# Attention and ternary feed-forward layer on one core: the order of sixteen matmuls inside each half of the probabilities-times-values product

## The chip, the cores and the metric

The kernel runs on one core of one Trainium2 chip. The metric is device time in microseconds (us) of one execution. Besides the plain timed executions there is one execution recorded by the hardware profiler, and every row below is from it. The engines are named as the profile names them: PE is TensorE (matmuls), PEld its loading of stationary operands, DVE is VectorE, ACT is ScalarE, POOL is GpSimd, and SP issues the DMAs.

## What is computed

The input x is 2048 rows of 256. It is normalised by layernorm, and the output is x plus an attention over it plus a feed-forward layer over it:

```
xn = layernorm(x)
qkv = einsum('bsd,ed->bse', xn, Wqkv)            # 16 heads of 128, q, k and v
logits = einsum('bqhd,bkhd->bhqk', q, k) * 128 ** -0.5
w = softmax(logits)
out = einsum('bhqk,bkhd->bqhd', w, v)
attn = einsum('bse,de->bsd', out, Wout)
hidden = sigmoid(xn @ quant(w1).T) * (xn @ quant(w2).T)   # 704 wide, weights -1, 0, 1
result = x + attn + hidden @ quant(w3).T
```

To keep float32 accuracy the operands of the matmuls are split in a high part, rounded to the matmul's type, and a low part, the rest. A product of two split operands is then three matmuls: high by high, high by low, low by high.

## The kernel before, in words

The feed-forward layer comes first and ends about 100 us into the span. Then come the 16 heads, each taking some 112 us. All of the program's order is written out by hand: each engine has its own list of instructions and waits for semaphores of the others.

Inside a head the 2048 queries are 16 tiles of 128 (`t`), and two tiles are a pair (`p`). For one tile PE computes the logits against all 2048 keys in two halves (`logits`, lines 349 to 351, twelve matmuls of 512 columns over the tile). DVE takes the row maximum (line 826), ACT the exponentials (line 629), DVE turns blocks of 32 by 32 (line 836), and DMAs move these blocks so that the keys lie on the partitions. ACT then rounds the high part (line 623) and POOL subtracts for the low part (line 967), both into `parts`. `parts` holds, for each of 16 blocks of 128 keys (`kb`), 256 columns of low parts (index 0) and 256 of high parts (index 1), for the 256 queries of a pair.

The function that the change touches is `products(half)`: it multiplies the values by the probabilities for half of the keys, that is 8 of the blocks. For each block it issues one matmul of 512 columns, `v_hi` by low and high parts together (line 357, into `ps_pv`, one whole bank of PSUM), and one of 256 columns, `v_lo` by the high parts alone (line 359, into `ps_pv_hi`, the second half of the same bank). Every one has its own stationary operand, so each matmul is preceded by a weight load. The last of the sixteen raises the semaphore `s_pv`, for which ACT waits before it reads the product (line 615) and before it writes the next pair into the same half of `parts` (line 623).

PE's list, which is what sets the order around the change, repeats every two tiles:

- at an odd tile: logits (12 matmuls), the output projection of an earlier pair (lines 367 to 369, six matmuls of 256 columns), and the first half's products of the next pair;
- at an even tile: logits (12), at one of them also a values projection ahead of the products (line 339, six matmuls), then the second half's products, and at most of them a projection of queries or values behind it (lines 329 and 339, six matmuls of 512 columns).

So `products` is called 256 times: 16 heads, 8 pairs, 2 halves. Half of the calls follow matmuls of 512 columns and half follow the six of 256 columns. Each head but the last ends with the next head's keys (line 320, 24 matmuls of 512 columns).

Of the kernel before, what the change touches and what calls it, by code (L numbers as in the profile page):

```python
# [43 lines left out]
KH = HALF // P  # L44
# [24 lines left out]
def build(nc, x_d, wqkv_d, wo_d, w1_d, w2_d, w3_d, out_d):  # L69
    ctx = ExitStack()  # L70
    with ctx:
# [242 lines left out]
        def _(pe):  # L314
# [40 lines left out]
            def products(half):  # L355
                for kb in range(half * KH, half * KH + KH):
                    nc.tensor.matmul(ps_pv, v_hi[:, kb, :], parts[:, kb].rearrange("p s a q -> p (s a q)"),  # L357
                                     start=(kb == 0), stop=False, skip_group_check=True)
                    last = nc.tensor.matmul(ps_pv_hi, v_lo[:, kb, :], parts[:, kb, 1].rearrange("p a q -> p (a q)"),  # L359
                                            start=False, stop=(kb == T - 1), skip_group_check=True)  # L360
                last.then_inc(s_pv, 1)
# [83 lines left out]
            def product_step(h, p, half, first=False):  # L445
                pe.wait_ge(s_pl, count(16, h, 2 * p + half + 1))
                if half == 0 and (p >= 1 or not first):
                    pe.wait_ge(s_olo, count(8, h, p))
                if p == 0:
                    pe.wait_ge(s_vlo, count(2, h, half + 1))  # L450
                products(half)
# [584 lines left out]
```

## Time and profile before

| | |
|---|---|
| median of 3 executions | 1926.77 us (1925.68 to 1930.1) |
| the profiled execution, its own time | 1927.86 us |
| span in the profile, first to last instruction | 1926.0 us |
| PE busy | 1874.0 us, 97% |
| DVE busy | 1648.2 us, 86% |
| POOL busy | 1359.7 us, 71% |
| ACT busy | 1253.0 us, 65% |
| DMA, mean busy share | 66.6% of 16 engines |

The span is 1.86 us shorter than that execution's time. A matmul's own duration in the profile (0.40 us for 512 columns, 0.28 us for 256) overlaps the next one's, since matmuls are pipelined. What a matmul costs in a stream is the distance from its start to the start of the next one, its pitch. The timeline shows starts to 0.01 us, so pitches are best read over several matmuls.

### The profile page before, as it was taken

The page shows a single profiled execution, that of the slowest core. Times are in us where ns is not written, and L with a number is a line of the kernel's source. Part 1 is how long each engine was busy: PE and PEld are TensorE (multiplying, and loading weights), DVE is VectorE, ACT ScalarE, POOL GpSimd, SP SyncE. Part 2 cuts the span into 40 slices and gives each one's busy share as a digit, 9 for nine tenths or more (in the row PEclk, how much of TensorE's full clock was granted, in tenths as well). Part 3 has the DMA queues.
Part 4 walks back from the last instruction along what each step waited for, and adds up shares of the span by engine and source line. Part 5 has one row for each costly group of instructions (what it writes and reads, how often), then busy time and mean ns, then how long its engine had stood idle before and what let it go on. Part 6 is the DMA issues. An engine that isn't in the chain of part 4 may idle for free.

```text
span 1926.0 us, 29406 instructions
## 1 busy us (share of the span) xinstructions
PE 1874.0 (97%) x9508; PEld 1582.4 (82%) x9508; DVE 1648.2 (86%) x2216; ACT 1253.0 (65%) x1698; POOL 1359.7 (71%) x514
## 2 busy tenths in 40 slices
PE   5979999999999999999999999999999999999997
PEld 4858888888888888888888888888888888888885
DVE  6368898898989899898989989898998989899894
ACT  3446676666767676666767666676766667666663
POOL 2418687776868777686878768686876768687676
PEclk9999999999999999999999999999999999999998
DMA  3036677676767767676776767677676767767675
GB/s 105 1 90 159 157 167 177 152 170 159 171 157 173 172 151 172 159 168 159 166 179 151 171 159 169 159 163 182 148 173 157 170 161 163 175 148 177 148 165 141
DMA packets 197108, 300.70 MB, mean 156 GB/s; under 512 B 38144, under 2 KB 57280, under 8 KB 197056
## 3 DMA queue, kind: packets, MB, share of 16 engines
q1 hardware_dynamic: 197056, 300.11, 66.6%
q8 instruction: 20, 0.33, 0.1%
q14 instruction: 32, 0.26, 0.0%
HBM read 12.65 MB, written 2.10 MB: 8 GB/s over the span
## 4 chain that ended last, share of the span: by engine, by line
PE 88%; SPq 3%; DVE 3%; POOL 2%; ACT 1%; DMA 1%; issue 1%; DVEq 0%; POOLq 0%; ACTq 0%
PE ps_o L357 23%; PE ps_o L359 12%; PE ps_s L349 11%; PE ps_s L351 11%; PE ps_s L350 11%; PE ps_t L339 4%; PE ps_s L320 4%; PE ps_t L329 4%; SPq L266 3%; PE ps_s L392 2%; PE ps_o L367 1%; PE ps_o L369 1%; PE ps_o L368 1%; POOL parts L967 1%; DVE prob L836 1%
## 5 line engine op out<-in xcount | busy, mean ns | idle before, releaser
L967 POOL TENSOR_TENSOR parts<-raw,parts 128x2048 fp32r<-128x2048 f32 x256 | 1185.3, 4631 | 454.6 <-ACT parts L623 453.8
L629 ACT ACTIVATE prob<-ps_s,neg_max 128x1024 f32<-128x1024 f32 x512 | 567.0, 1114 | 471.2 <-DVE neg_max L830 471.2
L357 PE MATMUL ps_o<-parts,v_hi 128*128 128x512 f32 x2048 | 739.7, 399 | 8.7 <-POOL parts L967 5.1
L826 DVE TENSOR_REDUCE row_max<-ps_s 128x1 f32<-128x1024 f32 x512 | 612.3, 1212 | 71.0 <-PE ps_s L351 51.6
L836 DVE STREAM_TRANSPOSE prob<-prob 128x1024 f32<-128x1024 f32 x512 | 604.3, 1218 | 58.5 <-ACT prob L629 58.0
L359 PE MATMUL ps_o<-parts,v_lo 128*128 128x256 f32 x2048 | 578.0, 282 | 0.0
L623 ACT CAST parts<-raw 128x2048 fp32r<-128x2048 f32 x256 | 490.5, 1916 | 99.7 <-DMA raw<-prob 96.4
L357 PEld LDWEIGHTS ps_o<-parts,v_hi 128*128 128x128 f32 x2048 | 387.8, 189 | 99.9 <-POOL parts L967 6.1
L349 PE MATMUL ps_s<-k_hi,q_hi 128*128 128x512 f32 x1024 | 404.0, 395 | 12.6 <-ACT prob L629 11.8
L351 PE MATMUL ps_s<-k_hi,q_lo 128*128 128x512 f32 x1024 | 400.3, 391 | 0.0
L350 PE MATMUL ps_s<-k_lo,q_hi 128*128 128x512 f32 x1024 | 399.8, 390 | 0.0
L359 PEld LDWEIGHTS ps_o<-parts,v_lo 128*128 128x128 f32 x2048 | 387.5, 189 | 4.3
L349 PEld LDWEIGHTS ps_s<-k_hi,q_hi 128*128 128x128 f32 x1024 | 192.5, 188 | 63.4 <-ACT prob L629 11.5
L351 PEld LDWEIGHTS ps_s<-k_hi,q_lo 128*128 128x128 f32 x1024 | 192.6, 188 | 42.7
L350 PEld LDWEIGHTS ps_s<-k_lo,q_hi 128*128 128x128 f32 x1024 | 192.8, 188 | 36.2
L853 DVE SCALAR_TENSOR_TENSOR y<-ps_o,inv_denom,y 128x256 f32<-128x256 f32 x256 | 111.0, 475 | 3.4 <-PE ps_o L369 3.4
L629 ACT ACTIVATION_READ_ACCUMULATOR prob<-ps_s,neg_max 128x1 f32 x512 | 99.3, 194 | 0.0
L329 PE MATMUL ps_t<-xt_hi,w_sp 128*128 128x512 f32 x256 | 90.5, 394 | 0.0
L339 PE MATMUL ps_t<-xt_hi,w_sp 128*128 128x512 f32 x256 | 90.1, 393 | 0.0
L840 DVE TENSOR_TENSOR o_lo<-ps_o,o_hi 128x256 fp32r<-128x256 f32 x128 | 54.3, 424 | 40.9 <-ACT o_hi L615 28.6
L320 PE MATMUL ps_s<-xt_hi,w_sp 128*128 128x512 f32 x256 | 81.8, 390 | 0.0
L367 PE MATMUL ps_o<-wo_hi,o_hi 128*128 128x256 f32 x256 | 72.3, 283 | 5.0 <-DVE o_lo L842 5.0
(94 smaller groups left out, 1599.1 us busy)
## 6 DMA issues: line engine op xcount, KB each, us to landing
raw<-prob SPq DMA_DIRECT2D x2048, 128.0 KB, 2.4
v_raw<-v_turned SPq DMA_DIRECT2D x244, 64.0 KB, 2.0
w_raw<-wqkv_dram SPq DMA_DIRECT2D x32, 128.0 KB, 2.5
y<-x_dram SPq DMA_DIRECT2D x4, 512.0 KB, 5.8
wo_raw<-wqkv_dram SPq DMA_DIRECT2D x16, 128.0 KB, 2.5
wo_raw<-wo_dram SPq DMA_DIRECT2D x16, 128.0 KB, 2.3
out_dram<-y SPq DMA_DIRECT2D x8, 256.0 KB, 2.9
w_raw<-w_dram SPq DMA_DIRECT2D x2, 704.0 KB, 10.1
```

Of the source, the lines that this page charges most:

```text
L329: last = nc.tensor.matmul(dst, w_sp[:, 0, c, w, :], x[:, c, col], start=(n == 0), stop=(n == 3 * C - 1))
L339: last = nc.tensor.matmul(dst, w_sp[:, 2, c, w, :], x[:, c, j * 512:(j + 1) * 512], start=(n == 0), stop=(n == 3 * C - 1))
L349: nc.tensor.matmul(ps_s[:, bank, :], q_hi[:, qb, tile], k_hi[:, col], start=True, stop=False)
L350: nc.tensor.matmul(ps_s[:, bank, :], q_hi[:, qb, tile], k_lo[:, col], start=False, stop=False)
L351: last = nc.tensor.matmul(ps_s[:, bank, :], q_lo[:, qb, tile], k_hi[:, col], start=False, stop=True)
L357: nc.tensor.matmul(ps_pv, v_hi[:, kb, :], parts[:, kb].rearrange("p s a q -> p (s a q)"), start=(kb == 0), stop=False, skip_group_check=True)
L359: last = nc.tensor.matmul(ps_pv_hi, v_lo[:, kb, :], parts[:, kb, 1].rearrange("p a q -> p (a q)"), start=False, stop=(kb == T - 1), skip_g ...
L623: nc.scalar.copy(half_of(1, half), moved(p, half)).then_inc(s_ph, 1)
L629: nc.scalar.activation(prob[:, t % E_RING, half * HALF:(half + 1) * HALF], ps_s[:, 2 * half:2 * half + 2, :].rearrange("p b n -> p (b n)") ...
L826: nc.vector.reduce_max(row_max[:, t, half:half + 1], ps_s[:, 2 * half:2 * half + 2, :].rearrange("p b n -> p (b n)"), AX_X).then_inc(s_mx, 1)
L836: nc.vector.transpose(tile, tile).then_inc(s_xp, 1)
L967: nc.gpsimd.tensor_tensor(half_of(0, half), moved(p, half), half_of(1, half), ALU.subtract).then_inc(s_pl, 1)
```

## The change

Inside one call of `products` the same sixteen matmuls are issued in another order: the loop over the eight blocks is now two loops. All eight of line 357 come first, then all eight of the former line 359, now line 360. The semaphore is still raised by the last one, the waits stand ahead of the first one as before, and nothing else in the program is changed; the lines behind it move down by one.

```diff
                 for kb in range(half * KH, half * KH + KH):
                     nc.tensor.matmul(ps_pv, v_hi[:, kb, :], parts[:, kb].rearrange("p s a q -> p (s a q)"),
                                      start=(kb == 0), stop=False, skip_group_check=True)
+                for kb in range(half * KH, half * KH + KH):
                     last = nc.tensor.matmul(ps_pv_hi, v_lo[:, kb, :], parts[:, kb, 1].rearrange("p a q -> p (a q)"),
                                             start=False, stop=(kb == T - 1), skip_group_check=True)
                 last.then_inc(s_pv, 1)
```

On PE, in the first head, the end of an output projection, then the start of a call of `products` before the change:

```order
L367 MATMUL ps_o<-wo_hi,o_hi 128x256
L368 MATMUL ps_o<-wo_lo,o_hi 128x256
L369 MATMUL ps_o<-wo_hi,o_lo 128x256
L357 MATMUL ps_o<-parts,v_hi 128x512 [waits output_low_ready,pt_low_ready]
L359 MATMUL ps_o<-parts,v_lo 128x256
L357 MATMUL ps_o<-parts,v_hi 128x512
L359 MATMUL ps_o<-parts,v_lo 128x256
```

The same place with the change, where x7 and x8 are equal instructions in a row and all lines from 359 on are one higher:

```order
L368 MATMUL ps_o<-wo_hi,o_hi 128x256
L369 MATMUL ps_o<-wo_lo,o_hi 128x256
L370 MATMUL ps_o<-wo_hi,o_lo 128x256
L357 MATMUL ps_o<-parts,v_hi 128x512 [waits output_low_ready,pt_low_ready]
L357 MATMUL ps_o<-parts,v_hi 128x512 x7
L360 MATMUL ps_o<-parts,v_lo 128x256 x8
L349 MATMUL ps_s<-k_hi,q_hi 128x512 [waits exponentials_ready,queries_low_ready]
```

The sixteen stand between the same neighbours and behind the same wait; only their inner order has moved. On DVE, ACT, POOL and SP no instruction has moved.

## Rows read from the trace of the kernel before

**Rows 1.** The page's first part: busy time, share, count of each engine.
```profile
PE 1874.0 (97%) x9508; PEld 1582.4 (82%) x9508; DVE 1648.2 (86%) x2216; ACT 1253.0 (65%) x1698; POOL 1359.7 (71%) x514
```

**Rows 2.** Windows; busy us (count) of PE, PEld, DVE, ACT, POOL; clock, DMA.
```profile
165.00:820.00 655.00, 654.54 (x3333) 553.85 (x3332) 585.07 (x775) 444.55 (x599) 482.42 (x176) 1.00 0.71 164
820.00:1800.00 980.00, 979.12 (x4987) 828.21 (x4986) 875.18 (x1159) 663.34 (x894) 726.85 (x263) 1.00 0.71 165
```

**Rows 3.** Waits of PE: total us, times, longest us.
```profile
PE ps_s L349 <- ACT prob L629: 11.8, 7, 3.0
PE ps_o L357 <- POOL parts L967: 5.1, 3, 2.5
PE ps_o L367 <- DVE o_lo L842: 5.0, 3, 2.3
```

**Rows 4.** Groups by line, 165 to 1820 us: busy us, mean ns; idle before.
```profile
L357 PE MATMUL ps_o<-parts,v_hi 128*128 128x512 f32 x1899 | 680.7, 397 | 0.5 <-POOL v_lo L960 0.5
L826 DVE TENSOR_REDUCE row_max<-ps_s 128x1 f32<-128x1024 f32 x474 | 566.8, 1212 | 63.1 <-PE ps_s L351 45.0
```

**Rows 5.** Timeline of PE, a call behind 512 columns: start us, duration us, what.
```profile
864.72 0.39 PE L357 MATMUL ps_o<-parts,v_hi 128*128 128x512 f32 x1
864.95 0.28 PE L359 MATMUL ps_o<-parts,v_lo 128*128 128x256 f32 x1
865.07 0.39 PE L357 MATMUL ps_o<-parts,v_hi 128*128 128x512 f32 x1
865.30 0.28 PE L359 MATMUL ps_o<-parts,v_lo 128*128 128x256 f32 x1
...
867.54 0.39 PE L329 MATMUL ps_t<-xt_hi,w_sp 128*128 128x512 f32 x1
```

**Rows 6.** Timeline of PE, a call behind the output projection.
```profile
872.36 0.40 PE L357 MATMUL ps_o<-parts,v_hi 128*128 128x512 f32 x1
872.60 0.28 PE L359 MATMUL ps_o<-parts,v_lo 128*128 128x256 f32 x1
...
873.07 0.39 PE L357 MATMUL ps_o<-parts,v_hi 128*128 128x512 f32 x1
873.30 0.28 PE L359 MATMUL ps_o<-parts,v_lo 128*128 128x256 f32 x1
...
875.18 0.39 PE L349 MATMUL ps_s<-k_hi,q_hi 128*128 128x512 f32 x1
```

**Rows 7.** Timeline of PE between them: ninth 512-column matmul, first of 256 columns.
```profile
869.38 0.39 PE L351 MATMUL ps_s<-k_hi,q_lo 128*128 128x512 f32 x1
...
871.65 0.28 PE L367 MATMUL ps_o<-wo_hi,o_hi 128*128 128x256 f32 x1
```

**Rows 8.** Timeline of PE, feed-forward: 48 of 256 columns, then 48 of 512.
```profile
60.56 0.28 PE L403 MATMUL ps_t<-w_q,hid_hi 128*128 128x256 f32 x1
...
66.25 0.39 PE L392 MATMUL ps_s<-xt_hi,w_q 128*128 x1
...
77.30 0.28 PE L403 MATMUL ps_t<-w_q,hid_hi 128*128 128x256 f32 x1
```

**Rows 9.** Timeline of the weight loads, output projection.
```profile
872.00 0.19 PEld L368 LDWEIGHTS ps_o<-wo_lo,o_hi 128*128 128x128 f32 x1
872.12 0.19 PEld L369 LDWEIGHTS ps_o<-wo_hi,o_lo 128*128 128x128 f32 x1
```

**Rows 10.** Timeline of ACT: the exponential ahead of the logits at 875.18.
```profile
873.36 1.12 ACT L629 ACTIVATE prob<-ps_s,neg_max 128x1024 f32<-128x1024 f32 x1 [1.50 <-DVE neg_max L830]
```

**Rows 11.** Timeline of PE, keys (24 of line 320) from first to the next line.
```profile
99.73 0.40 PE L320 MATMUL ps_s<-xt_hi,w_sp 128*128 128x512 f32 x1
...
105.19 0.39 PE L329 MATMUL ps_t<-xt_hi,w_sp 128*128 128x512 f32 x1
...
888.40 0.39 PE L320 MATMUL ps_s<-xt_hi,w_sp 128*128 128x512 f32 x1
...
893.88 0.39 PE L349 MATMUL ps_s<-k_hi,q_hi 128*128 128x512 f32 x1
```

## The prediction

> **What bounds the kernel now.** I read the busy shares first, then a table of long windows, then who waits for whom, and last the timeline of PE, matmul by matmul.
>
> PE is busy 97% of the span, DVE 86% [rows 1]. From 165 to 1800 us the reader is to see that PE is busy 1633.66 of 1635 us, with its clock granted in full, while DVE is busy 585.07 of 655 and 875.18 of 980 us, 89% in both [rows 2]. PE's waits for other engines are few: 7, 3 and 3 of them, 21.9 us together [rows 3], and of all that only 0.5 us stands before line 357 between 165 and 1820 us [rows 4]. So over 85% of the span there is one bound: the sum of PE's pitches. A busy share of 97% alone would not prove that, since matmul records overlap; what proves it is that the starts follow each other without a hole. The question is therefore whether the order of sixteen matmuls changes their pitches, and it has to be read from starts, not from durations.
>
> **The change part by part.** It removes no matmul, adds none, moves no wait, no semaphore and no DMA. The one term is the time of a call of `products`, and there are two kinds of call.
>
> Before, a call behind 512-column matmuls runs from 864.72 to 867.54, 2.82 us [rows 5], and one behind the output projection from 872.36 to 875.18, again 2.82 us [rows 6]. Both are eight pairs of 512 and 256 columns, 0.353 us a pair.
>
> What do the two widths cost in streams of their own? Between the two calls stand eighteen matmuls of 512 columns. From the ninth, at 869.38, to the first of 256 columns at 871.65 there are ten pitches in 2.27 us, 0.227 us each [rows 7]. The eight ahead of those, directly behind the alternating group, take 869.38 - 867.54 = 1.84 us, 0.230 us each [rows 5, 7]. So behind 256-column work the long ones need some time to settle at 0.227. The six of 256 columns take 872.36 - 871.65 = 0.71 us, 0.118 us each [rows 6, 7]; the 48 of the feed-forward layer take 66.25 - 60.56 = 5.69 us, 0.1185 us each [rows 8]. A pair in streams costs 0.227 + 0.118 = 0.345 us and in alternation 0.353 us: alternating costs about 8 ns a pair. It is the 512-column matmul that pays it: in the rows it stands at 0.23 to 0.24 us and the short one at 0.12.
>
> The new call behind 512-column matmuls: the stream before it is already settled, so 8 x 0.227 = 1.816, and 8 x 0.1185 = 0.948, together 2.764 us. Saved: 2.82 - 2.764 = 0.056 us.
>
> The new call behind the output projection: the eight long ones come right behind 256-column work, so I take the unsettled 0.230, 1.84 us, and 0.948 again, 2.788 us. Saved: 0.032 us.
>
> The two together are 0.088 us every two tiles, 0.044 us a call on average. Not every call counts. Between 165 and 1820 us there are 1899 matmuls of line 357, 237 calls [rows 4], where PE has no cover. The other 19 lie in the first and last head, where PE waits for others [rows 3] and what it saves may only lengthen a wait. I count them as nothing; in full they would be 0.8 us. The sum is 237 x 0.044 = 10.4 us.
>
> Bounds of that term. The trace shows no stream of line 357, so its pitch there is bounded by rows of others. The high end: the 48 matmuls of 512 columns in the feed-forward layer stay at 0.230 us (77.30 - 66.25 = 11.05 us) and never settle lower [rows 8]. With 0.230 in both kinds of call each saves 0.032, together 7.6 us. The low end: 0.227 in both kinds saves 0.056 a call, 13.3 us. To that may come something behind the call: 24 key matmuls behind a stream of 256 columns take 105.19 - 99.73 = 5.46 us, and behind an alternating group 893.88 - 888.40 = 5.48 us [rows 11]. So the work behind a call may settle 0.02 us sooner, for 237 calls 4.7 us; with it the low end is 18 us. I take nothing for it, because 0.02 us is the difference of two single readings to 0.01 us.
>
> Do eight short matmuls in a row expose their weight loads? A load is recorded at 0.19 us, longer than the pitch of 0.12 us, and the next load starts 0.12 us after it [rows 9]. So a load's record is a latency that overlaps, and streams of short matmuls with a new load each already run at 0.118 [rows 6 to 8]. I charge nothing. All eight short ones add into the same 256 columns; the output projection does so three in a row, within that same 0.118.
>
> Is there cover that goes away? The nearest deadline is the exponential that the next tile's logits wait for. It ended at 873.36 + 1.12 = 874.48, and the logits started at 875.18 [rows 10, 6]: 0.70 us to spare, against some 0.06 us that PE comes earlier. DVE is late next, but it still waits for PE's logits, 45.0 us in 165 to 1820 us [rows 4], which over 118 pairs of tiles is 0.38 us each, more than 0.088. The waits of PE itself, 21.9 us, stay.
>
> The sum stands against the profiled execution: 1927.86 - 10.4 = 1917.5 us. That execution lies 1.09 us above the median of the runs shown, 1926.77, so what I predict for a median is 1916.4 us.
>
> **The rivals.**
>
> The pitch belongs to line 357, not to the order. Its matmuls read `parts` and load `v_hi`, which no other line does, and in the alternating group most stand at 0.235 us. If they do so in a row, a call is 8 x 0.235 + 0.948 = 2.828 us, and 256 calls are 2 us longer: 1928.8, no measurable change. For it: that I have no stream of this line. Against it: two of the matmuls in the rows, at 865.07 and 873.07, have a pitch of 0.23 and not 0.24 [rows 5, 6], so the operands don't forbid it. A rule bears on this. The Trainium skill (TensorE: Matmul & The Clock Gate, "Back-to-back issue gap") gives the distance between isolated matmuls at full clock as columns over 2.4 GHz plus 2.5 ns, whatever stands beside them. By that rule a pair would cost 325 ns in any order and the change nothing, 1926.8 us. The rows disagree with its size, 353 ns in alternation, and with its independence, since the streams add up to 345.
>
> DVE takes over. It is busy 89% of the time, and its list is a chain of its own. If its 0.38 us of slack in a pair of tiles is bridged by some other wait, PE's saving turns into a new wait of line 349 for the exponentials, and the time stays at 1926.8. For it: the high share. Against it: DVE's wait for PE comes back at every odd tile, so the two stay in step.
>
> Slower: eight long reads of `parts` in a row. The long matmul directly behind the output projection has the longest pitch of all in the rows, 872.36 to 872.60, 0.24 us [rows 6]. If that is what line 357 costs when the reader before it is not relieved by a short matmul, for instance because ACT and POOL write the other half of `parts` at the time, a call becomes 8 x 0.24 + 0.948 = 2.868 us, 0.048 more, and 256 calls 12.3 us more: 1939.1 us. It turns slower from a pitch of 0.234 us on. Against it: in alternation a long one reads `parts` two thirds of the time already, without a steady 0.24.
>
> **How the numbers follow.** What can be told from no change here is 0.2%, 3.9 us. I give the forecast 0.82, the pitch of the line itself 0.07, DVE taking over 0.05, and the slower case 0.06. The forecast's own range is its bounds, 7.6 to 18 us off the median, 1909 to 1919. The range that should hold the time 8 times in 10 goes a little further on both sides, from 1908.5 to 1922, where part of a gain is swallowed by waits at the heads' ends. The two cases without an effect and the slower one, 0.18 together, are left outside. Faster by over 0.2%: 0.82, within it: 0.12, slower: 0.06.
>
> **What would show each step.** In the timeline of the kernel after, behind 512 columns: eight starts of line 357 at 0.227 us and eight of line 360 at about 0.12, the call 2.76 us long; behind the projection 2.79 us. The window from 165 to 1800 us still has PE busy all the time, with more matmuls in the same 980 us: 4987 now, and 0.5% more is 25. The waits of line 349 stay near 11.8 us. The forecast is wrong if line 357 in a row stands at 0.235 or above, if PE shows new waits for ACT in the middle heads, or if line 360 has a pitch of 0.19, a load laid bare.

## The result: 0.45% faster, by 9.0 us

The changed kernel takes 1917.59 us (median of 6, 1916.14 to 1921.84), the kernel before 1926.59 us (median of 6, 1925.68 to 1930.1). The ratio is 0.9955, with a 95% interval of 0.994 to 0.9969. The prediction was 1916.4 us, from 1908.5 to 1922. The profiled execution of the changed kernel took 1921.41 us, one of the two long ones of the six, and has a span of 1919.6 us. The two profiled executions differ by 6.4 us, not by 9; where the rest lies is shown further down.

The busy times [rows 1] and the longer of the two windows [rows 2] of the kernel after, in the same columns:

```profile
PE 1864.8 (97%) x9508; PEld 1573.8 (82%) x9508; DVE 1648.4 (86%) x2216; ACT 1252.9 (65%) x1698; POOL 1356.6 (71%) x514
```
```profile
820.00:1800.00 980.00, 978.19 (x5007) 826.81 (x5006) 878.50 (x1164) 664.87 (x895) 727.27 (x265) 1.00 0.71 165
```

In the same 980 us PE issues 5007 matmuls instead of 4987, 0.4% more. But its idle time there has doubled, from 0.9 to 1.8 us. That is small, and it is the first sign of something that was not in the forecast. The waits of PE [rows 3] show it as well; line numbers from 359 on are one higher:

```profile
PE ps_s L349 <- ACT prob L630: 12.5, 7, 3.0
PE ps_o L357 <- POOL v_lo L961: 5.8, 6, 2.0
```

The wait for the exponentials is about what it was. The one for `v_lo` was in the profile before too, and the forecast passed over it:

```profile
PE ps_o L357 <- POOL v_lo L960: 3.6, 3, 2.0
```

It stood at 3.6 us in 3 places and is now 5.8 us in 6.

Next the timeline of PE for the two kinds of call. Behind 512-column matmuls [rows 5]:

```profile
862.08 2.03 PE L357 MATMUL ps_o<-parts,v_hi 128*128 128x512 f32 x8
863.95 1.08 PE L360 MATMUL ps_o<-parts,v_lo 128*128 128x256 f32 x8
864.87 0.39 PE L329 MATMUL ps_t<-xt_hi,w_sp 128*128 128x512 f32 x1
...
877.99 0.39 PE L339 MATMUL ps_t<-xt_hi,w_sp 128*128 128x512 f32 x1
```

The call takes 864.87 - 862.08 = 2.79 us, before 2.82. The eight long ones take 1.87 us, 0.234 each; the eight short ones 0.92 us, 0.115 each. Behind the output projection [rows 6]:

```profile
869.67 0.40 PE L357 MATMUL ps_o<-parts,v_hi 128*128 128x512 f32 x1
...
872.47 0.39 PE L349 MATMUL ps_s<-k_hi,q_hi 128*128 128x512 f32 x1
```

2.80 us, before 2.82. A full period of two tiles, from one projection to the next, is 877.99 - 864.87 = 13.12 us. The same period of the kernel before, from the row at 867.54 [rows 5] to the next projection, is 13.22 us:

```profile
880.76 0.39 PE L339 MATMUL ps_t<-xt_hi,w_sp 128*128 128x512 f32 x1
```

So 0.10 us went. The rows show starts to 0.01 us, too coarse to say from one period where. Averaged over all periods of this form between 200 and 1760 us (68 in the trace before, 69 after), the period is 13.220 and 13.119 us. Of that difference 0.068 us lies inside the two calls: 2.823 to 2.785 us behind 512 columns, 2.823 to 2.793 us behind the output projection. The other 0.033 us lies in the 30 matmuls of 512 columns behind them. Inside the calls the long matmuls kept their average pitch, 0.234 us in both orders. It is the short ones that became cheaper, from 0.1185 to 0.115 us.

### The profile page after: what moved, and what is told of

It reads as the page before. It is cut to its first block, busy times and chain, and to the rows that moved or that the text cites. A ratio compares the mean times of both kernels' runs of the same rounds, so it can differ in the third digit from the quotient of the medians.

```text
span 1919.6 us, 29406 instructions
## 1 busy us (share of the span) xinstructions
PE 1864.8 (97%) x9508; PEld 1573.8 (82%) x9508; DVE 1648.4 (86%) x2216; ACT 1252.9 (65%) x1698; POOL 1356.6 (71%) x514
## 4 chain that ended last, share of the span: by engine, by line
PE 77%; POOL 6%; SPq 5%; issue 4%; DVE 4%; ACT 2%; DMA 2%; POOLq 0%; DVEq 0%; ACTq 0%
PE ps_o L357 20%; PE ps_o L360 10%; PE ps_s L349 10%; PE ps_s L350 10%; PE ps_s L351 10%; SPq L266 5%; POOL parts L968 5%; PE ps_t L339 4%; PE ps_s L320 4%; PE ps_t L329 4%; PE ps_s L393 2%; DVE prob L837 1%; PE ps_o L368 1%; PE ps_o L370 1%; PE ps_o L369 1%
## 5 line engine op out<-in xcount | busy, mean ns | idle before, releaser
L357 PE MATMUL ps_o<-parts,v_hi 128*128 128x512 f32 x2048 | 527.6, 399 | 10.0 <-POOL v_lo L961 5.8
L357 PEld LDWEIGHTS ps_o<-parts,v_hi 128*128 128x128 f32 x2048 | 376.8, 189 | 96.7 <-issue 6.0
L360 PEld LDWEIGHTS ps_o<-parts,v_lo 128*128 128x128 f32 x2048 | 274.2, 188 | 23.9
L360 PE MATMUL ps_o<-parts,v_lo 128*128 128x256 f32 x2048 | 277.4, 278 | 0.0
```

## The experiments

Each kernel is the changed one with one edit, unless the text says it starts from the one before. Times are medians; the kernel before, run beside them on the same chip, took 1925.5 to 1926.1 us.

**1. The wait for v_lo between the long and the short matmuls.** The reason is the new wait above. It is an edit that the new order makes possible, since the long ones don't read `v_lo`. Only the first pair of a head (`p == 0`) has this wait.

```diff
-            def products(half):
+            def products(half, low_ready=None):
                 for kb in range(half * KH, half * KH + KH):
                     nc.tensor.matmul(ps_pv, v_hi[:, kb, :], ...)
+                if low_ready is not None:
+                    pe.wait_ge(s_vlo, low_ready)
                 for kb in range(half * KH, half * KH + KH):
...
                 if p == 0:
-                    pe.wait_ge(s_vlo, count(2, h, half + 1))
+                    pe.wait_ge(s_vhi, count(2, h, half + 1))
-                products(half)
+                products(half, count(2, h, half + 1) if p == 0 else None)
```

> The changed kernel, but in the first pair of a head the wait for v_lo stands between the eight long matmuls and the eight short ones (ahead of the long ones only v_hi is waited for). Theory C (POOL's burst of parts, v_lo, parts, v_lo, parts, wo_lo at tiles 5 to 7 of every head sets three deadlines, and the faster PE now runs into them, 0.27 us a head): the stalls ahead of line 357 at tiles 5 and 6 go, but POOL still finishes wo_lo at the same moment, so the wait ahead of the output projection at tile 7 grows by about what they gave: 0 to 1 us faster than the changed kernel, 1917 us. Rival P (the pitches alone explain the 9 us, those stalls are no real cover that ran out): the same time as the changed kernel with no new wait anywhere, and the stalls at tiles 5 and 6 stay. Rival Q (each stall costs by itself): 2 to 3 us faster, 1915 us.

Measured: 1917.43 us (5 runs), ratio 0.9955 (0.9941 to 0.9969), the changed kernel's own. To see why, first POOL in the changed kernel, tiles 5 to 7 of one head:

```profile
920.96 4.64 POOL L968 TENSOR_TENSOR parts<-raw,parts 128x2048 fp32r<-128x2048 f32 x1 [2.47 <-ACT parts L624]
925.57 2.41 POOL L961 TENSOR_TENSOR v_lo<-v_raw,v_hi 128x1024 fp32r<-128x1024 f32 x1
927.95 4.61 POOL L968 TENSOR_TENSOR parts<-raw,parts 128x2048 fp32r<-128x2048 f32 x1
932.52 2.39 POOL L961 TENSOR_TENSOR v_lo<-v_raw,v_hi 128x1024 fp32r<-128x1024 f32 x1
...
935.03 4.60 POOL L968 TENSOR_TENSOR parts<-raw,parts 128x2048 fp32r<-128x2048 f32 x1
939.60 0.73 POOL L947 TENSOR_TENSOR wo_lo<-wo_raw,wo_hi 128x256 fp32r<-128x256 f32 x1
```

and PE at the three places that need what POOL makes there:

```profile
928.03 2.13 PE L357 MATMUL ps_o<-parts,v_hi 128*128 128x512 f32 x8
...
935.02 0.68 PE L357 MATMUL ps_o<-parts,v_hi 128*128 128x512 f32 x2
...
940.37 0.39 PE L351 MATMUL ps_s<-k_hi,q_lo 128*128 128x512 f32 x1
940.59 0.38 PE L368 MATMUL ps_o<-wo_hi,o_hi 128*128 128x256 f32 x1
```

POOL works without a pause from 920.96 to past 940.33. It ends `v_lo` at 927.98, and line 357 starts at 928.03, 0.05 us later and 0.20 us behind the matmul before it, instead of 0.12; the second half at 934.91, and line 357 starts at 935.02, where the first of the two has a pitch of 0.29 us instead of 0.234; `wo_lo` at 940.33, and the projection starts at 940.59 with its first matmul at a pitch of 0.22 us instead of 0.12. Three times PE has just been waiting for POOL. In experiment 1 the first two waits are gone, and the third stays:

```profile
935.58 0.76 POOL L949 TENSOR_TENSOR wo_lo<-wo_raw,wo_hi 128x256 fp32r<-128x256 f32 x1
```
```profile
936.19 0.39 PE L351 MATMUL ps_s<-k_hi,q_lo 128*128 128x512 f32 x1
936.56 0.38 PE L370 MATMUL ps_o<-wo_hi,o_hi 128*128 128x256 f32 x1
```

`wo_lo` ends at 936.34 and the projection comes 0.37 us behind the last logits instead of 0.22. What the first two gave, the third took.

**2. All three relieved.** The edit of experiment 1, and POOL makes `wo_lo` before the pair's first subtraction:

```diff
+                    if r == 3:
+                        wo_low(h)
                     if r >= 2:
                         low(h, r - 2, 0)
...
-                    if r == 3:
-                        wo_low(h)
```

> As the run with the wait for v_lo between the loops, and POOL computes wo_lo ahead of the pair's first subtraction at tile 6 instead of behind it. Theory C: all three deadlines of a head are off the path, 0.27 us a head come back, 14 middle heads: 3 to 4 us faster than the changed kernel, about 1914 us, a middle head 110.75 us instead of 111.04. Rival P: the same time as the changed kernel, 1917.6 us, middle head 111.04. Rival Q: the same as the run before it, 1915.

Measured: 1911.7 us (5 runs, 1910.89 to 1912.53), ratio 0.9922 (0.9909 to 0.9936). The gain is larger than expected, 5.9 us and not 3 to 4. No wait of PE is left between 165 and 1770 us. This head took 111.08 us in the changed kernel, from its first key matmul to that of the next head (885.59 to 996.67), and is 110.75 us here (880.18 to 990.93).

The other 2 us are two heads, the second and the last but one, in which POOL's burst ended over 1 us later than in a middle head of the changed kernel, and PE waited for it: 112.09 and 112.27 us there, 111.29 and 111.12 us here. This kernel beats both others.

**3 and 4. Less work for POOL, with the new order and with the old.** Both leave out seven eighths of `v_lo` in all heads but the first, so that part keeps the first head's numbers:

```diff
-            def values_low(h, half):
+            def values_low(h, half, full):
...
+                if not full:
+                    kb = slice(half * KH, half * KH + 1)
```

> The changed kernel in which POOL subtracts only one of eight blocks for v_lo in all heads but the first (the rest of v_lo is left as the first head's): POOL's burst is 4 us shorter per head. Theory C: no stall at tiles 5 to 7 any more, 3 to 4 us faster than the changed kernel, about 1914 us. Rival P: the same as the changed kernel, 1917.6 us.

> The kernel before with the same part of v_lo left out. Theory C: only some 0.06 us of stall a head are there to lose, so 0.5 to 1.5 us faster than the kernel before, 1925.5 us, and the run beside it is 11 to 12.5 us faster than this one: 0.10 us for every two tiles, 8 pairs, 15 heads. Rival P: the difference between the two stays the 9 us of the change.

Measured: 1913.62 us (ratio 0.9935, 0.9921 to 0.9948) with the new order, 1924.28 us (0.999, 0.9981 to 0.9999) with the old. The difference is 10.7 us. In these two the middle heads are all alike, 110.73 against 111.53 us: 0.80 us a head, 8 periods of 0.10. So this is what the order is worth when nothing else binds. With POOL's full work the same head of the two kernels differs by 111.56 - 111.08 = 0.48 us. The cover that ran out costs a middle head 0.3 us.

The sum over the second to the fifteenth head, from the first key matmul of the second to that of the sixteenth, leaves the ends of the program out:

| | order before | order after | difference |
|---|---|---|---|
| all of `v_lo` (before, after) | 1563.1 us | 1557.1 us | 6.0 us |
| an eighth of it (experiments 4, 3) | 1562.0 us | 1551.1 us | 10.9 us |

In experiment 2, with all of POOL's work but in another order, the same 14 heads take 1551.3 us. So in these heads the order was worth 10.9 us, and waits for POOL took some 5 us of it back.

**5. Four long, four short, twice.**

```diff
-                for kb in range(half * KH, half * KH + KH):
+                for quarter in (0, 1):
+                  for kb in range(half * KH + 4 * quarter, half * KH + 4 * quarter + 4):
                     nc.tensor.matmul(ps_pv, v_hi[:, kb, :], ...)
-                for kb in range(half * KH, half * KH + KH):
+                  for kb in range(half * KH + 4 * quarter, half * KH + 4 * quarter + 4):
                     last = nc.tensor.matmul(ps_pv_hi, v_lo[:, kb, :], ...)
```

> The changed order in two portions: four long, four short, four long, four short. If the cost lies in the switching between widths, the call is between both: from 2.79 us towards 2.82, with the four short ones after each switch at 0.122, 0.116, 0.114, 0.113 as in the changed kernel, and the long ones at 0.233 throughout: 2 x (4 x 0.233 + 0.465) = 2.79 us, the same as the changed kernel, since the first short ones are the only dear ones and a switch costs 10 ns. If the long row itself is what pays (eight in a row needed), the call stays at 2.82 us. Time 1918 by the first, 1926 by the second.

Measured: 1918.64 us, ratio 0.9964 (0.995 to 0.9978). The timeline of a call:

```profile
858.77 1.09 PE L358 MATMUL ps_o<-parts,v_hi 128*128 128x512 f32 x4
859.70 0.63 PE L361 MATMUL ps_o<-parts,v_lo 128*128 128x256 f32 x4
860.17 1.09 PE L358 MATMUL ps_o<-parts,v_hi 128*128 128x512 f32 x4
861.10 0.62 PE L361 MATMUL ps_o<-parts,v_lo 128*128 128x256 f32 x4
861.55 0.39 PE L329 MATMUL ps_t<-xt_hi,w_sp 128*128 128x512 f32 x1
```

2.78 us, and the long ones again at 0.93 / 4 = 0.233. Groups of four are enough; a change of width every fourth matmul costs nothing that can be read.

**6 and 7. Other operands for the long matmuls.** The moving one, then the stationary one (the outputs are then other numbers):

```diff
-nc.tensor.matmul(ps_pv, v_hi[:, kb, :], parts[:, kb]...,
+nc.tensor.matmul(ps_pv, v_hi[:, kb, :], xt_hi[:, kb % 2, kb // 2 % 4 * 512:kb // 2 % 4 * 512 + 512],
```
```diff
-nc.tensor.matmul(ps_pv, v_hi[:, kb, :], parts[:, kb]...,
+nc.tensor.matmul(ps_pv, xt_hi[:, 1, kb * P:(kb + 1) * P], parts[:, kb]...,
```

> The changed kernel in which the moving operand of line 357 is 512 columns of xt_hi (the operand of the projections) instead of parts, so the products come from other data. Theory A (the pitch of 0.233 us of line 357 in a row comes from reading parts): it falls to 0.227, the call to about 2.74 us. Theory B (it comes from the weight v_hi or from the place it adds into): it stays 0.233.

> The changed kernel in which the stationary operand of line 357 is 128 columns of xt_hi instead of v_hi, so the products come from other data. Theory A (reading parts sets 0.233 us): the pitch stays 0.233. Theory B (the weight load of v_hi): it falls to 0.227.

Measured (one execution each, 1921.02 and 1919.28 us): with `xt_hi` moving the long ones are at 1.82 / 8 = 0.2275, with `xt_hi` stationary at 1.87 / 8 = 0.234. So the pitch of 0.234 goes with reading `parts`. But the short ones behind the `xt_hi` reads went the other way, from 0.115 to 0.1175. Experiment 6:

```profile
860.28 1.98 PE L357 MATMUL ps_o<-xt_hi,v_hi 128*128 128x512 f32 x8
862.10 1.10 PE L360 MATMUL ps_o<-parts,v_lo 128*128 128x256 f32 x8
863.04 0.39 PE L329 MATMUL ps_t<-xt_hi,w_sp 128*128 128x512 f32 x1
...
876.18 0.39 PE L339 MATMUL ps_t<-xt_hi,w_sp 128*128 128x512 f32 x1
```

The call is down to 2.76 us, and yet the period is 13.14 us, not shorter than 13.12: the logits behind it lost what the call won. Theory A is right on the pitch and useless for the time.

**8. The old order on other operands.** The kernel before with experiment 6's edit.

> The kernel before, alternating, with the moving operand of line 357 replaced by 512 columns of xt_hi (its products come from other data). With the stream of long matmuls on xt_hi this completes the table of order by operand. If alternating itself costs (order), a pair stays near 0.353 us and the call at 2.82 against 2.76 us of the stream on the same operand. If the dear pair came from reading parts (operand), the pair falls to 0.345 and the call to 2.76 in either order.

Measured (one execution): 1919.54 us. The call is 862.56 - 859.76 = 2.80 us, the period 875.70 - 862.56 = 13.14 us.

```profile
859.76 0.39 PE L357 MATMUL ps_o<-xt_hi,v_hi 128*128 128x512 f32 x1
...
862.56 0.39 PE L329 MATMUL ps_t<-xt_hi,w_sp 128*128 128x512 f32 x1
...
875.70 0.39 PE L339 MATMUL ps_t<-xt_hi,w_sp 128*128 128x512 f32 x1
```

Neither expectation fits: the call fell, though not to 2.76, and the period fell nearly all the way. Alternating widths is not dear by itself: on `xt_hi` both orders have the same period. It is dear where both matmuls of a pair read `parts`, and there the short one reads again half of the columns that the long one has just read; whether it is the same tensor or the same columns, no run tells apart.

**9 and 10. `parts` at another place.**

```diff
+        pad = sb("pad", [P, 16])
         parts = sb("parts", [P, T, 2, 8, BLK], F32R)
```
and, for the second, the line of `parts` moved ahead of that of `prob`.

> The changed kernel with parts starting 64 bytes further on in every partition. If the long pitch of 0.233 us comes from how the address of parts stands to that of the weights within a short period, it changes, to 0.227 or to more. If it comes from something else of parts, it stays 0.233 and the time 1917 to 1918 us.

> The changed kernel with parts ahead of prob and raw, 64 KB lower in every partition. If the region of SBUF in which parts lies sets its pitch (the operands that stream at 0.227 us, xt_hi and k_hi, lie low), the long pitch falls towards 0.227. Otherwise 0.233 and 1917 to 1918 us.

Measured (one execution each): 1919.41 and 1918.37 us. 64 KB lower nothing changes (0.234 and 0.115). 64 bytes on, the pitches change, to 0.2275 and 0.119, and the period does not, 874.89 - 861.77 = 13.12 us. So it is reading `parts` where it stands, and not reading it at all, that goes with 0.234:

```profile
859.00 1.98 PE L358 MATMUL ps_o<-parts,v_hi 128*128 128x512 f32 x8
860.82 1.12 PE L361 MATMUL ps_o<-parts,v_lo 128*128 128x256 f32 x8
861.77 0.40 PE L330 MATMUL ps_t<-xt_hi,w_sp 128*128 128x512 f32 x1
...
874.89 0.40 PE L340 MATMUL ps_t<-xt_hi,w_sp 128*128 128x512 f32 x1
```

**11. Short ones first.**

```diff
+                blocks = list(range(half * KH, half * KH + KH))
+                if half == 0:
+                    long(blocks.pop(0))
                 for kb in range(half * KH, half * KH + KH):
                     nc.tensor.matmul(ps_pv_hi, v_lo[:, kb, :], ...)
+                for kb in blocks:
+                    last = long(kb)
...
```

(`long(kb)` issues the 512-column matmul of line 357, whose own loop is gone.)

> The changed kernel with the eight short matmuls ahead of the long ones (in the first half behind the first long one, which has to open the bank). The number of changes of width a call is the same. If the cost is one of changing width, the period of two tiles stays 13.12 us. If it is the settling of long matmuls behind short ones, the logits behind the call start settled (2.72 us for twelve instead of 2.735) but the long ones of the call are unsettled in both kinds of call: within 0.03 us of 13.12 us.

Measured (one execution): 1925.18 us. The call is 2.82 us, the period 865.29 - 852.08 = 13.21 us, nearly all of the gain gone. This was expected by neither.

```profile
852.08 0.40 PE L339 MATMUL ps_t<-xt_hi,w_sp 128*128 128x512 f32 x1
...
862.47 1.10 PE L364 MATMUL ps_o<-parts,v_lo 128*128 128x256 f32 x8
863.41 2.03 PE L357 MATMUL ps_o<-parts,v_hi 128*128 128x512 f32 x8
865.29 0.40 PE L329 MATMUL ps_t<-xt_hi,w_sp 128*128 128x512 f32 x1
```

The long ones are at 0.235 as in the changed kernel, the short ones at 0.1175. They are at 0.115 only where they stand behind long ones that read `parts` at its own place.

**12. The kernel before with `parts` 64 bytes on.** The pad of experiment 9 alone.

> The kernel before, alternating, with nothing changed but that parts starts 64 bytes further on in every partition. Theory S (the dear pair is one of the steady patterns into which loads and matmuls fall, and where operands start decides between them; the order is only one way to leave it): the pair falls from 0.353 to about 0.350 us or less, the period of two tiles from 13.22 to about 13.13 us, the time to about 1918 us like the regrouped kernel. Theory O (alternating widths on parts is dear by itself): 13.22 us and 1926 us, as before.

Measured: 1928.54 us (11 runs), ratio 1.0013 (1.0004 to 1.0022); the period is 877.23 - 864.00 = 13.23 us.

```profile
861.19 0.39 PE L358 MATMUL ps_o<-parts,v_hi 128*128 128x512 f32 x1
...
864.00 0.40 PE L330 MATMUL ps_t<-xt_hi,w_sp 128*128 128x512 f32 x1
...
877.23 0.40 PE L340 MATMUL ps_t<-xt_hi,w_sp 128*128 128x512 f32 x1
```

Theory S falls: moving `parts` does not help the old order. The order does, at both places tried.

In one table, the call behind 512 columns, and the period of two tiles, both in us, each read once. The averages over the 68 or 69 periods between 200 and 1760 us of each trace are within 0.01 us of these:

| order, what the long ones read | call | period |
|---|---|---|
| alternating, parts | 2.82 | 13.22 |
| alternating, parts 64 bytes on | 2.81 | 13.23 |
| alternating, xt_hi | 2.80 | 13.14 |
| short first, parts | 2.82 | 13.21 |
| long first, parts | 2.79 | 13.12 |
| long first, parts 64 bytes on | 2.77 | 13.12 |
| long first, xt_hi | 2.76 | 13.14 |

## Why the prediction was right, and where its steps were not

**The bound** was read rightly: PE's pitches set the time of the middle heads, and the order acts through them, by 0.10 us in each period of two tiles.

**The call** was mis-sized, and the saving in it was put on the wrong matmuls. I took 0.227 for a long one and 0.1185 for a short one from streams of other lines. They are 0.234 and 0.115. The sum let the long ones fall from their pitch in alternation to 0.227; they did not fall, on average 0.234 us in both orders. Nearly all of the saving is the eight short ones, 0.030 us a call, and no row of the kernel before foretold it. By my own reckoning a long one at 0.234 leaves no gain, so that the call gained at all is luck as far as this step goes. The rival that the pitch belongs to line 357 had the long one right, 0.235, and the wrong end, since it kept 0.1185 for the short ones. Saved per call are 0.038 and 0.030 us on average, where I had 0.056 and 0.032.

**Behind the call** I took nothing, and named up to 0.02 us a call as a bound. It is 0.033 us in a period of two calls, inside that bound. So the pitches give 0.10 us a period where the sum had 0.088: 0.020 less than in the sum inside the calls, 0.033 more than in the sum behind them. The two errors nearly cancel.

**The cover** is the step that failed. I asked for the nearest deadline, left out the wait for `v_lo` when I listed PE's waits, looked at the logits' wait for the exponentials (0.70 us to spare, and it did hold), and took that for all of PE's waits. A sum over a repeating period says nothing on a place that comes once a head. There POOL makes `v_lo` twice and `wo_lo` once beside its usual work, and PE was close behind it already. In the kernel before POOL ended the first of the two at 928.41 + 2.41 = 930.82 us, and the call that needs it started at 931.02:

```profile
928.41 2.41 POOL L960 TENSOR_TENSOR v_lo<-v_raw,v_hi 128x1024 fp32r<-128x1024 f32 x1
```
```profile
931.02 0.40 PE L357 MATMUL ps_o<-parts,v_hi 128*128 128x512 f32 x1
```

0.20 us to spare; the second half and `wo_lo` had 0.19 and 0.33 us (937.77 to 937.96 and 943.20 to 943.53). The new order brings PE 0.28 us forward by the first of them: without a wait there, in experiment 1, the call starts 42.34 us behind the head's first key matmul, and before 42.62 us. POOL does not come forward with it: `v_lo` ends 42.42 us behind that matmul before and 42.39 us with the change. Experiment 1 shows that the waits are linked, 2 and 3 what they cost: a middle head gained 0.48 us instead of 0.80, and 14 heads 6.0 us instead of 10.9. The rival on another engine taking over named the wrong engine: I looked at DVE, the busiest after PE at 89%, and it was POOL at 74%. A mean share hides a burst.

**The slower case**, 0.24 us for a long one in a row, did not come: it is 0.234, as in alternation.

**The median and the profile.** From the end of the feed-forward layer's work to the last head's keys the two profiled executions differ by 6.5 us. The first head takes 118.84 us before and 118.28 after. In experiment 5, whose periods are those of the changed kernel, it takes 115.51, and the rows of the windows show the clock beside it, first the changed kernel, then experiment 5:

```profile
108.00:132.00 24.00, 17.58 (x73) 13.21 (x72) 17.73 (x20) 8.33 (x15) 0.93 (x2) 1.00 0.38 90
132.00:152.00 20.00, 12.80 (x44) 9.83 (x44) 16.01 (x17) 12.88 (x17) 11.22 (x4) 0.83 0.68 155
```
```profile
108.00:132.00 24.00, 18.61 (x68) 14.10 (x67) 16.24 (x19) 7.75 (x15) 0.94 (x2) 0.86 0.40 95
132.00:152.00 20.00, 14.54 (x66) 11.20 (x64) 17.85 (x19) 14.00 (x18) 13.11 (x5) 1.00 0.65 150
```

In both, PE waits for the first exponentials in this part, and the granted clock then falls to the half level, 1.2 GHz, for 7 to 8 us in all. Where it comes later, part of it meets the first call of `products`, here the changed kernel, then experiment 5:

```profile
148.02 3.49 PE L357 MATMUL ps_o<-parts,v_hi 128*128 128x512 f32 x8 [2.01 <-POOL v_lo L961]
```
```profile
146.16 1.18 PE L358 MATMUL ps_o<-parts,v_hi 128*128 128x512 f32 x4 [0.53 <-POOL v_lo L962]
```

The next logits start at 152.43 and 149.04 us, so the call takes 4.41 against 2.88 us, and the wait ahead of it is 2.01 against 0.53 us. Together these are the 3 us. They are not set by the order: in the trace of experiment 12, with the old order, the first head took 115.68 us. The same 3 us probably separate the two long executions of the changed kernel, 1921.41 and 1921.84, from the other four, 1916.14 to 1918.02; only one of the six has a trace, so this was not shown. How much of the 9.0 us between the medians is the order, and how much an unequal share of such executions, stays open within that: between 6 and 9 us. So the total, 10.4 us forecast and 9.0 measured, agrees better than its steps do. Pitches right by two errors, a cover left out that cost some 5 us, and up to 3 us that may not be the order's stand between them; the close agreement is partly luck.

**A rule weighed.** The Trainium skill (TensorE: Matmul & The Clock Gate, "Back-to-back issue gap") makes the distance of isolated matmuls depend on their columns alone, an estimate of 216 and 109 ns for these by its formula. No matmul here stands alone, each having its own weight load, and no stream reached that: the least were 0.227 and 0.115 us. And sixteen matmuls of these widths took 2.76 to 2.82 us by order and operand, so the estimate is too low for this kernel and has no place for what the order does.

**What stays open** is why reading `parts` by both matmuls is dear in one order and not in the other, why the short ones are the cheaper for it, and why a saving inside the call can come back behind it (experiments 6 and 9). The runs show the table, not the mechanism: a shift by 64 bytes and the number of width changes do not decide, and what stands ahead of a short matmul does. No run took the weight loads apart from the matmuls, gave the two widths different banks to add into, or let the short one follow a long one on other columns of `parts`.

## What to carry to other kernels

Where PE is the bound and has no gaps, the order of unlike matmuls can be worth half a per cent, as it was here, but judge it by the period from one repeat to the next, never by the group that was edited: the pitches shift between the group and what follows. Before counting a gain on the busiest engine over many repeats, go once through everything that it waits for in a whole outer turn, and look for the place where another engine works without a pause, however low its mean share. If a wait can be moved behind work that doesn't need it, move all that depend on the same burst at once; relieving some of them only fills the next.

## What was not expected of the hardware

- Behind 512-column work the same long matmul in a row stood at 0.2275 or 0.234 us by the start of its moving operand, 64 bytes apart, and the short ones behind it at 0.119 or 0.115 us, while the period stayed at 13.12 us (experiment 9).
- Eight short matmuls behind eight long ones took 0.92 us, and ahead of them 0.94 us, with the same operands (experiment 11).
- The first head took 114.9 to 116.9 us in some traces and 118.3 to 118.8 us in others, of the old and the new order alike, and in the longer ones, and in the one of 116.9 us, the half clock stood in the window from 132 to 152 us.
